# Small stages of an eight-step pass dealt anew over the matrix engine's queue

## The chip, the cores and the metric

The kernel runs on one core of a Trainium2 chip. The metric is the device time of one execution in microseconds (us); lower is better. The core has a matrix engine (TensorE, PE in the profile, with its weight loads as PEld), VectorE (DVE), ScalarE (ACT), GpSimd (POOL) and SyncE (SP). Each works through its own queue in the written order, and they wait for one another by semaphores.

## The reference

Two transformer layers over x of 8 batches, 512 tokens, 128 features, with a layer norm ahead of each part:

```python
x = x + _L0_attn_ref(_layernorm(x), Wq, Wk, Wv, g_scale)   # 16 heads of 8; q, k to unit length
x = x + _L0_ffn_ref(_layernorm(x), ...)                    # top-1 of 8 experts, hidden 32, gelu
x = x + _L1_attn_ref(_layernorm(x), w_q, w_k, w_v, w_o)    # 16 heads of 64, causal
x = x + _L1_ffn_ref(_layernorm(x), ...)                    # top-2 of 8 experts, hidden 512, gelu
```

The first attention is softmax(g q k^T) v with unit q and k ("cosine" scores); the second is causal softmax(q k^T / 8) v and a projection. The first expert layer computes a hidden row with gelu for all experts, masks it by the chosen one, and multiplies by W2; the second sorts the rows by expert.

## The kernel before

Everything but the second expert layer runs in one software pipeline. `steps()` gives passes i = -3 to 8 of eight steps, p = 0 to 7. In a pass the second attention is at batch l1 = i, one **pair** of heads a step; the first expert layer is at batch f = i+1; the first attention at s = i+2, two **portions** (`cosine` 0 and 1, 128 keys of four heads each) a step; layer norm and projections of the first attention at h = i+3; and routing of the second expert layer at t = i-1. So passes -2 and -1 have portions but (nearly) no pairs, passes 0 to 5 have both, 6 and 7 have pairs alone. Behind the pipeline the second expert layer runs over sorted rows; the change doesn't touch it.

The order is written out by hand, once for each engine, in four loops over `steps()` that must agree. On PE a step is:

- `score_unit(g, 0)` and `max_unit(g+1, 0)`; `values0(c-1)`, the weighted values of the portion before;
- `values1(g-1)` in two halves, with `cosines(c)`, the scores of the step's first portion, between them;
- score and max unit 1, then small stages ("fills"); score and max unit 2; the q projection of pair g+2;
- more fills; `sums1` (denominators of pair g-1), `max_transposed` (row maxima of pair g+1), the k projection;
- `cosines(c+1)`, `values0(c)`, and a tail of fills, after which the next step begins.

Fills are, among others, `values1_rows` (the second attention's values, eight pieces (t, half) for a batch, three matmuls each), `transposes` to "xtT", "xh2T", "xnT", "xT0", "x2T", `logits0`, `hidden0`, `onehot_transposed`, `masks0` and `experts0_out` of the first expert layer, `qkv0` of the first attention, `group_operands` (its qT and kT), `projection_out`, and `logits1` and `ranks1` of the routing.

Two resources tie the order down. Score, max and cosine units alternate between two PSUM slots (`UNIT_NO`, from `unit_order`): a unit waits until the unit two before it has been read, by ACT's exponentials (`score_exp`, `cosine_exp`) or DVE's `maxima`. All projections and fills alternate between two other banks (`WORK_NO`, from `work_order`): `work_open` waits until the work two before it has been moved out:

```python
def work_open(pe, *name):
    pe.wait_ge(work_free[WORK_NO[name] % 2], work_fills(*name))
```

q and k are freed late: ACT writes their high part (`hi_part`, tile ra), then DVE the low part (`lo_part`, ra too, L1078). ACT has one activation table at a time; `hidden0_gelu` in step 3 loads the Gelu table, runs two Gelus, and loads the table of exponentials back. `group_rows`, `squares`, `unit_rows`, `variances`, `standardize`, `experts0_choice`, `routing1` are DVE stages. `parts_copied` (ACT) and `parts_split` (DVE) prepare `group_operands`.

## Time and profile before

| | before |
|---|---|
| time, median of 3 runs | 1633.49 us (1622.28 to 1648.9) |
| the profiled execution: its own time, its span | 1636.53 us, 1634.8 us |
| busy PE, PEld | 1327.0 us (81%), 798.3 us (49%) |
| busy DVE, ACT, POOL | 934.6 us (57%), 851.8 us (52%), 600.4 us (37%) |
| mean granted PE clock | 0.917 |

The span is the stretch that the profile shows instruction by instruction; the execution's own time is 1.7 us longer. A busy PE is one that has matmuls in its pipeline. Passes 0 to 7 lie between 167.77 us and 1365.60 us of the span, eight steps each; the pass taken as the sample below is pass 2, from 475.88 us to 632.78 us.

### The profile page before, as it was taken

What the parts mean: (1) busy time and instruction counts of PE and PEld (TensorE: products, weight loads), DVE (VectorE), ACT (ScalarE), POOL (GpSimd) and SP (SyncE); (2) the same over time, 40 slices, a digit from 0 to 9 for tenths busy, and PEclk for the clock granted to TensorE, in tenths of its full rate; (3) what the DMA queues carried; (4) which work ended last, traced back from release to release, by engine and by line L of the source; (5) the groups of instructions that cost most, each with busy time, mean ns of one, the idle gap of its engine ahead of it and who ended that gap; (6) DMA issues with size and microseconds to landing.
All of it is one profiled execution on the core that took longest, in us unless ns stands there. A gap on an engine that the chain in (4) does not pass through costs nothing.

```text
span 1634.8 us, 27815 instructions
## 1 busy us (share of the span) xinstructions
PE 1327.0 (81%) x9189; PEld 798.3 (49%) x9189; DVE 934.6 (57%) x3262; ACT 851.8 (52%) x1642; POOL 600.4 (37%) x768
## 2 busy tenths in 40 slices
PE   3878888988888789889988988988888884599970
PEld 1223444554455445545445444544555553488860
DVE  5355755565756576656555764555554654265655
ACT  3665665656565556555654665444424531255533
POOL 1010322233253335333423442235325444265554
PEclk7878999999999999989998999899979987699985
DMA  7060990000000000000000000001010000212222
GB/s 288 1 229 1 8 3 1 1 7 8 1 14 8 7 1 21 1 7 3 19 1 8 8 8 1 7 8 59 8 43 36 1 11 22 90 54 55 58 90 104
DMA packets 63051, 53.17 MB, mean 33 GB/s; under 512 B 39752, under 2 KB 49488, under 8 KB 62656
## 3 DMA queue, kind: packets, MB, share of 16 engines
q1 hardware_dynamic: 58592, 42.47, 13.2%
q0 software_dynamic: 4320, 8.92, 1.6%
q8 instruction: 78, 1.28, 0.3%
q14 instruction: 61, 0.50, 0.1%
HBM read 20.56 MB, written 30.81 MB: 31 GB/s over the span
## 4 chain that ended last, share of the span: by engine, by line
PE 59%; DVE 17%; ACT 14%; issue 7%; POOL 2%; DMA 1%; POOLq 1%; SPq 0%; DVEq 0%; ACTq 0%
PE scores L1529 10%; PE work L1469 8%; PE outs L1675 7%; PE outs L1548 6%; DVE scores L1085 5%; ACT a_buf L824 5%; PE work L1578 4%; PE scores L1498 3%; DVE ra L1078 3%; PE scores L1662 3%; PE work L1561 3%; ACT ra L830 3%; PE outs L1860 2%; ACT rsum L836 2%; PE work L1559 2%
## 5 line engine op out<-in xcount | busy, mean ns | idle before, releaser
L1085 DVE CUSTOM_DVE_ANT_0 scores<-scores,mask_qk 128x512 f32<-128x512 f32 (+3 forms) x512 | 239.3, 520 | 240.8 <-PE scores L1498 238.1
L824 ACT ACTIVATE a_buf<-scores 128x1024 f32<-128x1024 f32 x256 | 248.0, 1026 | 110.7 <-PE scores L1662 101.4
L676 POOL TENSOR_SCALAR_AFFINE_SELECT big<-big 128x256 f32<-128x256 f32 x256 | 100.9, 407 | 541.5 <-ACT big L818 540.7
L818 ACT ACTIVATE big<-scores 128x1024 f32<-128x1024 f32 (+1 forms) x192 | 169.2, 882 | 231.0 <-PE scores L1529 224.5
L1529 PE MATMUL scores<-ra 64*128 64x512 f32 (+3 forms) x1536 | 188.8, 352 | 47.2 <-ACT a_buf L824 33.0
L686 POOL TENSOR_TENSOR big<-big 128x768 f32<-128x768 f32 x64 | 118.6, 1854 | 191.2 <-PE work L1561 191.0
L1529 PEld LDWEIGHTS scores<-ra 64*128 64x128 f32 x1536 | 124.4, 193 | 109.4 <-ACT a_buf L824 42.3
L1548 PE MATMUL outs<-big 128*64 128x512 f32 (+3 forms) x1024 | 164.8, 449 | 2.2 <-DVE yT L1109 2.2
L1675 PE MATMUL outs<-a_buf 128*16 128x512 f32 x1024 | 148.4, 655 | 8.6 <-DVE wqkv_lo L1032 4.9
L1109 DVE TENSOR_TENSOR yT<-outs,rsum 128x512 f32<-128x512 f32 x64 | 44.3, 692 | 148.4 <-ACT rsum L841 148.4
L1548 PEld LDWEIGHTS outs<-big 128*64 128x64 f32 x1024 | 64.2, 137 | 115.9 <-issue 103.4
L973 ACT ACTIVATE big<-scores,b_sb 128x128 f32<-128x128 f32 x284 | 81.1, 368 | 74.8 <-PE scores L1850 43.5
L669 POOL TENSOR_TENSOR rstd<-var_eps,minus_half 128x4 f32<-128x4 f32 x48 | 50.5, 1052 | 161.9 <-DVE var_eps L1047 161.9
L830 ACT CAST ra<-work 128x512 fp32r<-128x512 f32 x128 | 75.0, 586 | 61.7 <-PE work L1469 59.3
L773 POOL DMA_INDIRECT choice_rows<-big x71 | 69.7, 982 | 81.6 <-DVE big L1410 79.7
L1078 DVE TENSOR_TENSOR ra<-work,ra 128x512 fp32r<-128x512 f32 x128 | 87.9, 687 | 18.1 <-ACT ra L830 12.7
L1498 PE MATMUL scores<-ra 64*128 64x512 f32 (+3 forms) x512 | 81.6, 355 | 14.1 <-DVE neg_max L1085 13.1
L836 ACT ACTIVATE rsum<-work 128x512 f32<-128x512 f32 x64 | 38.2, 597 | 101.7 <-PE work L1561 101.7
L1529 PE MATMUL scores<-neg_max_T,pick 64*128 64x512 f32 (+3 forms) x512 | 85.7, 329 | 0.0
L1662 PE MATMUL scores<-qkT 32*128 32x512 f32 x512 | 74.3, 516 | 12.8 <-ACT a_buf L824 10.5
L689 POOL TENSOR_TENSOR big<-big 128x512 f32<-128x512 f32 x64 | 82.4, 1288 | 5.0
L1469 PE MATMUL work<-x_hi,wqkv_hi 128*128 128x512 f32 x128 | 67.7, 529 | 20.0 <-ACT rsum L836 19.8
(216 smaller groups left out, 2600.7 us busy)
## 6 DMA issues: line engine op xcount, KB each, us to landing
sorted_rows<-xrows SPq DMA_DIRECT2D x33, 520.0 KB, 6.8
big<-sorted_rows SPq DMA_DIRECT2D x71, 65.0 KB
a_buf<-in_w SPq DMA_DIRECT2D x2, 2048.0 KB, 8.2
a_buf<-choice_rows SPq DMA_DIRECT2D x16, 256.0 KB, 4.9
a_buf<-in_x SPq DMA_DIRECT2D x8, 256.0 KB, 2.9
x_rows<-x SPq DMA_DIRECT2D x8, 256.0 KB, 2.0
ra<-x_rows SPq DMA_DIRECT2D x8, 256.0 KB
out<-a_buf SPq DMA_DIRECT2D x8, 256.0 KB, 2.0
```

The costliest lines, as they stand in the source:

```text
L686: nc.gpsimd.tensor_tensor(tsum, prob1(g, 0)[:, :, P:SEQ], prob1(g, 1)[:, :, 0:3 * P], ALU.add).then_inc(tsum_step, 1)
L818: activation(prob1(g, i), d[:, :, 0:256] if i == 2 else d, ACT.Exp, scale=SCALE1).then_inc(unit_free("pair", g, i), 1)
L824: activation(prob0(c)[:, i * 1024:(i + 1) * 1024], unit_wait(act, "cosine", c, i), ACT.Exp).then_inc(unit_free("cosine", c, i), 1)
L830: copy(dst[:, g % 2, :], w).then_inc(qk1_hi, 1)
L1078: v.tensor_tensor(lo[:, g % 2, :], w, hi[:, g % 2, :].bitcast(F32), ALU.subtract).then_inc(free_of(which, g), 1)
L1085: return v.tensor_tensor_reduce(scores_, scores_, mask_qk[:, SEQ - width:SEQ], -1.0, 3e38, ALU.add, ALU.min, neg_max[:, qt, j:j + 1])
L1469: last = mm(dst, a, c, start=(n == 0), stop=(n == 2))
L1498: last = mm(d[:, j * SEQ + at:j * SEQ + at + width], q_hi[heads(j), g % 2, qt * P:(qt + 1) * P], k_hi[heads(j), g % 2, 0:width], start=(n ...
L1529: last = mm(d[:, j * SEQ + at:j * SEQ + at + width], lhs, c[heads(j), g % 2, queries], start=(n == 0 and term == 0), stop=(n == len(blocks ...
L1548: last = mm(outs[heads(j), 0, kb * P:], v1[:, kb, n * D1:(n + 1) * D1], probs, start=(kb == 0), stop=(kb == TILES - 1))
L1662: last = mm(d[:, i * SEQ:(i + 1) * SEQ], qkT0[rows, 1, g % 2, kb * P:(kb + 1) * P], qkT0[rows, 0, g % 2, :], start=True, stop=True)
L1675: last = mm(outs[STRIP * j:STRIP * j + VCOLS, 1, :], vstat(s)[:, kb, g * HG + j, :], prob0(c)[:, j * SEQ:(j + 1) * SEQ], start=(kb == 0), ...
```

## The change

Only the order is changed; every stage remains, with the same operands. It does the following:

- **A new place for fills** right behind `values0(c-1)`, ahead of `values1`. In steps 0 to 7 it holds: v(3,0); v(1,1); lg0; nothing; both masks; qkv0 0 and 1; v(0,0); v(1,0).
- **At most one fill between q and the sums**: v(0,1); xtT; xh2T; xnT; lg1; qkv0 3; none; none.
- **Behind unit 1**: oT in the even steps, and v(2,1), v(3,1), qkv0 2, v(2,0) in the odd ones.
- **`values0(c)` moves** from behind `cosines(c+1)` to ahead of the k projection.
- **Step 3 (`GELU_STEP`)**: `cosines(c)` and its exponentials move behind score and max unit 1.
- **Tails**: ohT in step 3, xT0 in step 4 behind `experts0_out`, rank in step 5 behind x2T. On DVE `routing1` comes behind the additions of y0, `slots1` and `gates1` move to step 6, `unit_rows` to the middle of step 7. On ACT `parts_copied` moves from early in steps 1, 3, 5 to the end of steps 0, 2, 4, and in step 7 from early to behind the exponentials of unit 1; `inverse_norms` moves from the end of step 6 to early in step 7.

```diff
+GELU_STEP = 3
...
@@ unit_order
-        units += cosine(0) if i == 0 else []
+        units += cosine(0) if i == (1 if o.p == GELU_STEP else 0) else []
@@ scalar
-                if p in (1, 3, 5) and s is not None:
-                    parts_copied(s, p // 2 + 1)
-                if p == 7 and h is not None:
-                    parts_copied(h, 0)
-                if p == 3 and f is not None:
+                if p == GELU_STEP and f is not None:
                     hidden0_gelu(f)
...
+                if p == 7 and h is not None:
+                    inverse_norms(h)
-                if o.cosine(0) is not None:
+                if o.cosine(0) is not None and p != GELU_STEP:
                     cosine_exp(o.cosine(0))
...
+                if o.cosine(0) is not None and p == GELU_STEP:
+                    cosine_exp(o.cosine(0))
...
+                if p in (0, 2, 4) and s is not None:
+                    parts_copied(s, p // 2 + 1)
                 if (o.i, p) == (-2, 0):
                     weights_hi_parts()
@@ vector
-                if p == 4 and t is not None:
-                    routing1(t)
                 if p == 4 and f is not None:
                     for i in range(2):
                         w = work_wait(dve, "y0", f, i)
...
+                if p == 4 and t is not None:
+                    routing1(t)
@@ tensor
+                if p == 0 and l1 is not None:
+                    values1_rows(l1, 3, 0)
+                if p == 1 and l1 is not None:
+                    values1_rows(l1, 1, 1)
+                if p == 2 and f is not None:
+                    logits0(f)
+                if p == 4 and f is not None:
+                    masks0(f, 0)
+                    masks0(f, 1)
+                if p == 5 and h is not None:
+                    qkv0(h, 0)
+                    qkv0(h, 1)
...
                 if o.pair(1) is not None:
                     max_transposed(o.pair(1))
+                if o.cosine(0) is not None:
+                    values0(o.cosine(0))
                 if o.pair(2) is not None:
                     project("k", 1, o.pair(2))
                 if o.cosine(1) is not None:
                     cosines(o.cosine(1))
-                if o.cosine(0) is not None:
-                    values0(o.cosine(0))
```

**Step 3 on PE**, from `values0` to score unit 2, of the pass with i = 1; before (`scores<-qkT` is a portion's scores, `outs<-a_buf` is `values0`, `outs<-big` `values1`, `scores<-ra` score and max units, `work<-wqkv` a piece of v):

```order
506 L1675 MATMUL outs<-a_buf 16x512 x4
507 L1548 MATMUL outs<-big 64x512 x2
508 L1548 MATMUL outs<-big 64x384 x2
509 L1662 MATMUL scores<-qkT 128x512 x4
510 L1548 MATMUL outs<-big 64x256 x2
511 L1548 MATMUL outs<-big 64x128 x2
512 L1529 MATMUL scores<-ra 128x384 x6
```

and after:

```order
522 L1556 MATMUL outs<-big 64x128 x2
523 L1537 MATMUL scores<-ra 128x384 x6
524 L1537 MATMUL scores<-neg_max_T,pick 128x384 x2
525 L1537 MATMUL scores<-ra 128x128 x6
526 L1537 MATMUL scores<-neg_max_T,pick 128x128 x2
527 L1506 MATMUL scores<-ra 128x384 x2
528 L1506 MATMUL scores<-ra 128x128 x2
529 L1477 MATMUL work<-wqkv_hi,x_hi 128x512
530 L1477 MATMUL work<-wqkv_lo,x_hi 128x512
531 L1477 MATMUL work<-wqkv_hi,x_lo 128x512
532 L1670 MATMUL scores<-qkT 128x512 x4
533 L1537 MATMUL scores<-ra 128x256 x6
```

The portion's scores stood ahead of unit 1 and now stand behind it and a piece of v.

**The end of step 3 on PE**, from the denominators to the next step; before (`work<-big,ones` is `sums1`, L1509 `max_transposed`, L1469 the k projection, L1648 `group_operands`):

```order
529 L1559 MATMUL work<-big,ones 64x128 x2
530 L1561 MATMUL work<-big,ones 64x384 x2
531 L1509 MATMUL work<-ident_b,neg_max_hl 128x128 x4
532 L1469 MATMUL work<-x_hi,wqkv_hi 128x512
533 L1469 MATMUL work<-x_lo,wqkv_hi 128x512
534 L1469 MATMUL work<-x_hi,wqkv_lo 128x512
535 L1662 MATMUL scores<-qkT 128x512 x4
536 L1675 MATMUL outs<-a_buf 16x512 x4
537 L1648 MATMUL work<-ident_r,parts 128x128 x8
538 L1469 MATMUL work<-wqkv_hi,x_hi 128x512
```

and after:

```order
540 L1567 MATMUL work<-big,ones 64x128 x2
541 L1569 MATMUL work<-big,ones 64x384 x2
542 L1517 MATMUL work<-ident_b,neg_max_hl 128x128 x4
543 L1683 MATMUL outs<-a_buf 16x512 x4
544 L1477 MATMUL work<-x_hi,wqkv_hi 128x512
545 L1477 MATMUL work<-x_lo,wqkv_hi 128x512
546 L1477 MATMUL work<-x_hi,wqkv_lo 128x512
547 L1670 MATMUL scores<-qkT 128x512 x4
548 L1656 MATMUL work<-ident_r,parts 128x128 x8
549 L1621 MATMUL work<-ident_b,a_buf 8x128 x4
```

`values0` now stands ahead of the k projection, and the operands' transposes come straight behind the portion's scores.

**The first two steps of pass -2 on PE**, where there are no pairs; before:

```order
3 L1648 MATMUL work<-ident_r,parts 128x128 x8
4 L1662 MATMUL scores<-qkT 128x512 x8
5 L1675 MATMUL outs<-a_buf 16x512 x4
6 L1462 MATMUL outs<-bias_ln_sb,res 128x8 x2
7 L1675 MATMUL outs<-a_buf 16x512 x4
8 L1662 MATMUL scores<-qkT 128x512 x8
9 L1675 MATMUL outs<-a_buf 16x512 x4
```

and after:

```order
3 L1656 MATMUL work<-ident_r,parts 128x128 x8
4 L1670 MATMUL scores<-qkT 128x512 x4
5 L1683 MATMUL outs<-a_buf 16x512 x4
6 L1670 MATMUL scores<-qkT 128x512 x4
7 L1470 MATMUL outs<-bias_ln_sb,res 128x8 x2
8 L1683 MATMUL outs<-a_buf 16x512 x4
9 L1670 MATMUL scores<-qkT 128x512 x4
10 L1683 MATMUL outs<-a_buf 16x512 x4
```

The scores of two portions stood together (x8); now each is followed by its own `values0`.

**ACT in the same place**; before:

```order
18 L824 ACTIVATE a_buf<-scores 128x1024 x4
19 L802 CAST wqkv_hi<-yT 128x2048
20 L804 CAST wqkv_hi<-yT 128x1024
21 L852 CAST parts<-a_buf 128x4x16 x4
22 L852 CAST parts<-a_buf 128x8x8 x4
```

and after:

```order
18 L831 ACTIVATE a_buf<-scores 128x1024 x4
19 L859 CAST parts<-a_buf 128x4x16 x4
20 L859 CAST parts<-a_buf 128x8x8 x4
21 L809 CAST wqkv_hi<-yT 128x2048
22 L811 CAST wqkv_hi<-yT 128x1024
```

The copies of the parts now stand ahead of the high parts of the weights.

## Rows read from the trace of the kernel before

**Rows 1.** Page, part 4: the chain that ended last, shares of the span.
```profile
PE 59%; DVE 17%; ACT 14%; issue 7%; POOL 2%; DMA 1%; POOLq 1%; SPq 0%; DVEq 0%; ACTq 0%
```
**Rows 2.** Windows: steps 0 to 7 of pass 2; length, busy by engine, clock, DMA.
```profile
475.88:492.00 16.12, 14.07 (x108) 7.27 (x107) 8.62 (x27) 9.34 (x14) 8.83 (x12) 1.00 0.05 17
492.00:512.86 20.86, 18.85 (x145) 11.79 (x145) 14.62 (x62) 12.30 (x23) 8.44 (x10) 1.00 0.05 15
512.86:532.10 19.24, 17.11 (x124) 9.17 (x123) 11.49 (x42) 9.69 (x13) 6.37 (x8) 1.00 0.01 1
532.10:554.35 22.25, 17.32 (x121) 9.99 (x121) 12.84 (x50) 15.26 (x26) 7.53 (x9) 0.92 0.00 1
554.35:578.09 23.74, 20.11 (x150) 12.05 (x150) 14.56 (x51) 10.38 (x14) 6.89 (x11) 1.00 0.03 12
578.09:596.68 18.59, 16.46 (x119) 8.42 (x118) 11.45 (x48) 12.62 (x29) 6.38 (x8) 1.00 0.00 1
596.68:616.22 19.54, 17.74 (x138) 10.88 (x138) 15.45 (x46) 10.88 (x16) 7.63 (x9) 1.00 0.01 4
616.22:632.78 16.56, 15.00 (x114) 8.04 (x113) 8.29 (x31) 11.22 (x22) 7.69 (x10) 1.00 0.04 13
```
**Rows 3.** Timeline, step 1: start, length, engine, line; [idle before it <- what ended it].
```profile
502.11 0.39 PE L1469 MATMUL work<-wqkv_hi,x_hi 128*128 128x512 f32 x1
...
503.67 0.44 PE L1559 MATMUL work<-big,ones 128*64 128x128 f32 x4 [0.72 <-DVE ra L1078]
...
504.69 0.40 PE L1509 MATMUL work<-ident_b,neg_max_hl 128*128 128x128 bf16 x4
...
505.45 0.50 PE L1469 MATMUL work<-x_hi,wqkv_hi 128*128 128x512 f32 x1 [0.37 <-ACT rsum L836]
...
506.34 0.51 PE L1662 MATMUL scores<-qkT 32*128 32x512 f32 x4
...
506.78 1.05 PE L1675 MATMUL outs<-a_buf 128*16 128x512 f32 x8
...
506.93 1.95 ACT L824 ACTIVATE a_buf<-scores 128x1024 f32<-128x1024 f32 x2
507.12 0.68 DVE L1078 TENSOR_TENSOR ra<-work,ra 128x512 fp32r<-128x512 f32 x1
...
509.09 3.84 PE L1578 MATMUL work<-wo_sb,yT 128*128 128x128 f32 x32 [0.45 <-DVE qkT L1131]
```
**Rows 4.** Timeline, step 3: the Gelu on ACT and what PE waits for.
```profile
534.26 1.25 ACT L852 CAST parts<-a_buf 128x64 fp32r<-128x64 f32 x8
...
535.53 1.28 ACT L877 ACT_TABLE_LOAD   x1
...
536.82 1.26 ACT L877 ACTIVATE a_buf<-work,bias 128x512 f32<-128x512 f32 x2
...
539.40 1.94 ACT L824 ACTIVATE a_buf<-scores 128x1024 f32<-128x1024 f32 x2
...
540.47 1.16 PE L1529 MATMUL scores<-ra 64*128 64x384 f32 x6 [3.07 <-ACT a_buf L824]
```
**Rows 5.** Timeline, step 4: a transpose's wait, the routing's first row, the last fill's wait.
```profile
563.88 0.63 PE L1476 MATMUL work<-ident_r,a_buf 128*128 128x128 f32 x4 [1.45 <-DVE attn L1142]
...
572.67 0.18 DVE L1062 TENSOR_REDUCE top<-lg 128x4 f32<-128x32 f32 x1
...
577.27 0.89 PE L1588 MATMUL work<-wqkv_sb,a_buf 128*128 128x384 f32 x2 [0.25 <-DVE res L1332]
```
**Rows 6.** Timeline, pass -2: PE's wait for the weights, four exponentials in a row.
```profile
39.15 1.91 PE L1675 MATMUL outs<-a_buf 128*16 128x512 f32 x8 [4.86 <-DVE wqkv_lo L1032]
...
49.87 3.77 ACT L824 ACTIVATE a_buf<-scores 128x1024 f32<-128x1024 f32 x4 [4.19 <-PE scores L1662]
```
**Rows 7.** Windows: behind the Gelu's wait in pass 2, and step 4 of pass 3.
```profile
540.47:544.48 4.01, 4.01 (x23) 3.29 (x23) 1.21 (x5) 1.89 (x2) 0.65 (x2) 0.57 0.00 0
711.23:737.36 26.13, 22.97 (x149) 13.30 (x148) 14.30 (x51) 10.52 (x14) 6.91 (x11) 0.87 0.03 11
```

More of the change, by code:

```diff
@@ L101, in add @@
             names.extend(some)
-    if p in (0, 2, 4, 6):
-        b, g = (s, p // 2 - 1) if p else (f, GROUPS0 - 1)
-        add(b, ("oT", b, g))
-    if p == 1:
-        add(l1, ("v", l1, 0, 1))
-    if p == 3:
-        add(l1, ("v", l1, 2, 1))
-    if p == 4:
-        add(f, ("mask", f, 0))
-        add(h, ("xT0", h))
-    if p == 5:
-        add(t, ("rank", t))
-        add(h, ("qkv0", h, 1))
-    if p == 7:
-        add(f, ("v", f, 1, 0))
-    add(o.pair(2), ("q", o.pair(2)))
     if p == 0:
@@ L125, in work_order @@
     if p == 2:
-        add(f, ("xtT", f), ("xh2T", f))
-    if p == 3:
-        add(t, ("xnT", t))
-        add(f, ("ohT", f))
+        add(f, ("lg0", f))
     if p == 4:
-        add(f, ("mask", f, 1))
-        add(t, ("lg1", t))
+        add(f, ("mask", f, 0), ("mask", f, 1))
     if p == 5:
-        add(h, ("qkv0", h, 2), ("qkv0", h, 3))
+        add(h, ("qkv0", h, 0), ("qkv0", h, 1))
     if p == 6:
@@ L137, in work_order @@
     if p == 7:
-        add(f, ("v", f, 2, 0))
+        add(f, ("v", f, 1, 0))
+    if p in (0, 2, 4, 6):
+        b, g = (s, p // 2 - 1) if p else (f, GROUPS0 - 1)
+        add(b, ("oT", b, g))
+    if p == 1:
+        add(l1, ("v", l1, 2, 1))
+    if p == 3:
+        add(l1, ("v", l1, 3, 1))
+    if p == 5:
+        add(h, ("qkv0", h, 2))
+    if p == 7:
+        add(f, ("v", f, 2, 0))
+    add(o.pair(2), ("q", o.pair(2)))
+    if p == 0:
+        add(l1, ("v", l1, 0, 1))
+    if p == 1:
+        add(f, ("xtT", f))
+    if p == 2:
+        add(f, ("xh2T", f))
+    if p == 3:
+        add(t, ("xnT", t))
+    if p == 4:
+        add(t, ("lg1", t))
+    if p == 5:
+        add(h, ("qkv0", h, 3))
     add(o.pair(-1), ("sum", o.pair(-1)))
@@ L149, in work_order @@
     if p == 2:
-        add(f, ("lg0", f), ("hid0", f, 0), ("hid0", f, 1))
+        add(f, ("hid0", f, 0), ("hid0", f, 1))
     if p == 3:
-        add(l1, ("v", l1, 3, 1))
+        add(f, ("ohT", f))
     if p == 4:
         add(f, ("y0", f, 0), ("y0", f, 1))
-        add(h, ("qkv0", h, 0))
+        add(h, ("xT0", h))
     if p == 5:
         add(f, ("x2T", f))
+        add(t, ("rank", t))
     if p == 6:
@@ L1262, in _ @@
                     squares(h)
+                if p == 7 and h is not None:
+                    unit_rows(h)
                 if o.pair(1) is not None:
@@ L1313, in _ @@
                     work_moved(dve, "projB", t)
-                if p == 2 and f is not None:
-                    w = work_wait(dve, "lg0", f)
-                    v.tensor_copy(lg0[:], w[:, 0:TILES * EXPERTS].rearrange(
-                        "p (t e) -> p t e", e=EXPERTS)).then_inc(free_of("lg0", f), 1)
                 if p == 2 and t is not None:
@@ L1343, in _ @@
                                     ALU.subtract).then_inc(free_of("x2T", f), 1)
-                if p == 6 and h is not None:
-                    unit_rows(h)
+                if p == 5 and t is not None:
+                    ranks_moved(t)
+                if p == 6 and t is not None:
+                    slots1(t)
+                    gates1(t)
                 if p == 6 and l1 is not None:
@@ L1755, in _ @@
                     max_unit(o.pair(1), 2)
-                if p == 6 and f is not None:
-                    work_moved(pe, "x2T", f)
                 if o.pair(2) is not None:
@@ L1779, in _ @@
                 if p == 5 and h is not None:
-                    qkv0(h, 2)
                     qkv0(h, 3)
-                if p == 6 and f is not None:
-                    values1_rows(f, 0, 0)
-                if p == 7 and f is not None:
-                    values1_rows(f, 2, 0)
                 if o.pair(-1) is not None:
@@ L1793, in _ @@
                     cosines(o.cosine(1))
-                if o.cosine(0) is not None:
-                    values0(o.cosine(0))
                 if p in (1, 3, 5) and s is not None:
@@ L1810, in _ @@
                 if p == 4 and h is not None:
-                    qkv0(h, 0)
+                    pe.wait_ge(rows_ready["a0"], h + 1)
+                    transposes(rows_h, "xT0", h)
                 if p == 5 and f is not None:
@@ L1814, in _ @@
                     transposes(rows_a, "x2T", f)
+                if p == 5 and t is not None:
+                    ranks1(t)
                 if p == 6 and l1 is not None:
```

101 lines of the change are left out of this document (47 added, 54 removed).

## The prediction

> **What bounds the kernel now.** I read the chain of waits first [rows 1]: it runs over PE for 59% of the span, over DVE for 17% and over ACT for 14%. So PE's queue is the spine, and the rest is handshakes in which PE stands still for a DVE or ACT step. Next the windows of one pass, step by step [rows 2]: 156.9 us together, of which PE is busy 136.7 us. The 20.2 us left are spread over all steps (1.6 us in step 7, 2.1 in step 0), with two lumps: step 3 has 22.25 - 17.32 = 4.9 us and step 4 has 3.6 us. Then the timeline, to see what each hole is [rows 3 to 5]. In every step a few are the same:
>
> - q to sums: a fill starts at 502.11, the sums at 503.67, since with one fill between they share q's bank and wait for its low part on DVE. The hole is 1.56 us wide whatever fills it; a piece of v leaves 0.72 of it idle, so it costs about 0.84 [rows 3].
> - 0.37 us ahead of k, for the logarithm that frees the sums' bank [rows 3].
> - Behind unit 1, where PE waits for the exponentials of that unit: a hole of about a fill, filled in either kernel in most steps.
> - The Gelu step: ACT goes through parts 1.25, table 1.28, two Gelus 1.26, a table of the same length again, and only then the portion's exponentials, which PE's unit 1 needs: 3.07 us idle [rows 4].
>
> A hole is paid once, so a fill in it is free and the same fill elsewhere costs its length. That is how I price a change that only moves things. All step sums are against the lengths in [rows 2].
>
> **The change part by part.**
>
> *`values0(c)` ahead of k.* The transposed maxima start at 504.69 and k at 505.45, 0.76 us later with 0.37 idle [rows 3]. With `values0` between (the operands start 0.98 after it begins; its row says 1.05, modelled end), k starts 0.38 + 0.98 = 1.36 later: +0.60. The tail loses 0.98. Net -0.38 wherever the tail is pure work. But `values0` used to hide something: k's low part is done on DVE at 507.12 + 0.68 = 507.80, 2.35 us after k begins, and the second of the exponentials' halves later still [rows 3]. In a step with no tail (step 0) the next score unit waited for the first half of the exponentials before and waits as long now: they begin at 506.93, 1.48 behind k's start, one half is 0.97, so 2.5 to 2.7 us behind k in both kernels; there the move is a plain +0.6. With operands in the tail, kT waits for the low part, at 2.4 instead of 1.8 behind k. In step 1 the projection then waits for DVE's copy of qT, begun when the low part is done: 2.35 + 0.7 + 0.05 = 3.1 against 509.09 - 505.45 = 3.64: -0.54, after +0.6.
>
> *Fills behind the values.* Nothing is waited for there, so a fill costs its length: 0.8 for a piece of v, 0.9 for lg0, 0.7 for both masks, 1.7 for two pieces qkv0. It pays only where it empties a place in which it cost as much or more.
>
> Step by step:
> - Step 0: v(3,0) +0.8, v(0,1) is free in the q hole as v(3,0) was, `values0` +0.6: **+1.4**.
> - Step 1: v(1,1) +0.8, v(2,1) and xtT in holes, `values0` +0.6 - 0.54: **+0.9**.
> - Step 2: lg0 only changes place; xtT is gone from a q hole that held two fills (the second waits for the low part and then costs its length): -0.6; `values0` -0.38, and 0.1 back where the second hidden matmul waits for k's low part: **-0.9**.
> - Step 3: PE's unit 1 no longer waits. It starts at about 4.9 us of the step (540.47 - 532.10 = 8.4, less 3.07 idle, less 0.44 for the portion's scores). On ACT, with the parts gone, loads and Gelus end at 6.1, unit 1's exponential at 7.2. The portion's scores follow, and DVE must have read max unit 1 by 8.2. Then comes a new wait, with nothing of PE's between: the two exponentials of the portion [rows 4], the first free at 8.8 for score unit 2, the second at 9.8 for max unit 2. So I leave 1.6 us idle there, 1.0 in the later holes and 0.4 at the start. Work: 17.32, less v(2,1) 0.7, less 1.3 that the slower clock had added (below): 15.3. Sum 18.35: **-3.9**. Queued behind the late portion on ACT are unit 2's exponential and q's high part; both come in time, since q begins at 10.1.
> - Step 4: xT0 waited 1.45 us for DVE in the bank of oT [rows 5]; it now stands in the tail. The routing stood on DVE from 572.67 for 4 us ahead of the additions of y0, and PE's qkv0 came at 577.27 behind these [rows 5]; the additions now come first and PE doesn't wait for them. Work 20.11 less one qkv0 0.85 = 19.3, waits left 1.5 (unit 1 and 2 about 0.5, q hole 0.6, small ones): 20.8: **-2.9**. The routing still takes its 4 us, and holds DVE's first maxima of step 5 until 5.4 us of that step; they are needed there by the second half of the portion's scores at 5.9, since two qkv0 stand ahead. So it is covered by 0.5 us.
> - Step 5: work 16.46 + 0.85, waits 2.3 (rank at the end waits for DVE's copy of kT, 3.8 behind k): 19.6: **+1.0**.
> - Step 6: v(0,0) +0.8; no fill between q and sums, so the sums go at once, and only the maxima wait for the low part (q to k 3.8 instead of 4.1 with `values0` inside): -0.4; tail -1.0: **-0.6**.
> - Step 7: v(1,0) +0.8, same -0.4, kT's wait leaves the tail at 2.9 instead of 3.2; ACT's parts, 1.25, stand ahead of unit 2's exponential and delay q's high part by 0.2: **+0.4**.
>
> Sum -4.6 us a pass (156.9 to 152.3). Passes 0 to 5 are of this kind: **-27.6**. Passes 6 and 7 have no portions; fills at the new place cost there, the emptied holes pay: **-2**, between -6 and +4.
>
> *The start.* Passes -2 and -1 have portions and few pairs, so ACT's exponentials set the pace: four in a row, 3.77 us, when two portions' scores are issued together [rows 6]. Now the second portion's scores stand behind `values0` of the first, which waits for both its exponentials: per step ACT idles for 0.98 + 0.44 + 0.1, about 1.5 us, where no fills lie between. Four steps are light enough for the full price, but where qT and kT, weights or xT0 kept PE busy anyhow it is 0 to 1. Against that, step 7 of pass -2 no longer holds ACT behind the norms: I give it -3. One item is certain: in step 0 of pass -2 the weights' high parts come behind the later exponentials and the parts. PE already waits 4.86 us for them [rows 6]; later exponentials 2.5 plus parts 1.25: +3.7. The start in all: **+5.5**, between 0 and +18.
>
> *The clock.* Behind the 3.07 us wait the granted clock over 540.47 to 544.48 is 0.57 [rows 7], most of it at 1.2 GHz. That cost is in step 3 above. There is more: step 4 of pass 3 took 26.13 at 0.87, against 23.74 in pass 2 [rows 7]. I take four such losses of 2.4 us for passes 3 to 5. With fewer and shorter idle stretches I expect half of them gone: **-5**, between -10 and 0. The Trainium skill, TensorE: Matmul & The Clock Gate, Part 1, says that the throttled level is the default and that activity lifts it; the trace agrees in step 3, where a wait precedes the fall, but in step 4 of pass 3 no wait as long stands ahead.
>
> The sum: -27.6 - 2 + 5.5 - 5 = -29 us. The profiled execution is 1636.5 us, 3 us above the median of the runs, so it becomes 1607.4, and the median **1604 us** (-1.8%).
>
> A place where page and row differ: the switch of tables. The row shows 1.28 us and the Gelu starting right behind it [rows 4]. The Trainium skill, ScalarE: Activation LUTs, What ACT_TABLE_LOAD costs, adds a drain of 1380 ns to each switch. By that, the exponential of unit 1 in step 3 would end 2.8 us later and an estimated 2.8 x 6 = 17 us of the gain would be gone. The row decides, and I add nothing.
>
> **The rivals.**
>
> *A cleaner clock* (0.2): with the longest wait gone all losses of that kind vanish and the start is as cheap as its lower end: -27.6 - 4 + 1 - 10 = -41: 1593. For it: the fall in [rows 7] follows the wait. Against: the falls in later passes.
>
> *The Gelu step keeps DVE on the path* (0.12): ahead of the maxima of unit 1, which free the slot for the portion's second half, stand `experts0_choice` and the variances. If they end 2 us later than I reckon, everything behind shifts: -29 + 6 x 2 = -17: 1616. That would be the change not doing what it says.
>
> *The start at its worst* (0.12): 12 steps at 1.5 us, and a good part at half clock since PE idles more: -29 + 18 = -11: 1622.
>
> *Slower* (0.06): `values0` was a buffer behind k; without it there are bare waits of about 1 us behind k in steps 0, 1, 3, 5 and 7 and 1.6 us in step 3. If these drop the clock once or more a pass, each fall costs some 2.4 us (26.13 - 23.74) [rows 7]. The gain is used up at 29 / 2.4 = 12 falls, two a pass; at three a pass the sum is +14: 1647.
>
> **How the numbers follow.** The forecast has 0.5, and its own bounds (passes 6 and 7, the start, fill prices of 0.7 or 0.84 in four steps) are about 12 us to each side. The range holds the cleaner clock, the Gelu and the start's rivals: 1586 to 1632. 2%, about what a measurement of this kernel can tell from no change, is 32.7 us: faster means below 1600.8. All of the first rival and 0.4 of the forecast's half lie below: 0.40. Slower by over 2% needs 1666, past even the slow rival: 0.03. The rest 0.57.
>
> **What would show it.** The windows of a pass: 152 us in place of 157, step 3 at 18 to 19, step 4 at 21, but steps 0, 1 and 5 longer by 1 us each. The row of unit 1 in step 3 without a wait on ACT; in its place up to 1 us ahead of score unit 2. No 0.37 ahead of k; a wait of 0.5 ahead of kT. Pass -2 with exponentials in twos and the weights' wait above 8 us. If step 3 is still over 20, or the start over 10 us longer, or the granted clock below 0.9, the prediction is wrong at that term.

## The result: 1.8% slower, and where the time went

| | before | after |
|---|---|---|
| time, median | 1640.13 us (4 runs, 1622.28 to 1648.9) | 1657.93 us (4 runs, 1652.76 to 1662.49) |
| ratio, 95% interval | | 1.0184 (1.0099 to 1.0268) |
| profiled execution, its span | 1636.53, 1634.8 us | 1652.76, 1651.0 us |
| busy PE, DVE | 1327.0, 934.6 us | 1335.9, 966.5 us |
| mean granted PE clock | 0.917 | 0.909 |

The changed kernel is slower by 1.0 to 2.7%. (The ratios leave out executions in a slower state of the chip, so they differ from the quotients of the medians (1.011 here), and of one experiment, a_weights, the profiled execution was among those slower ones, so only its start is read from the trace.) The prediction said 1604 us with a range of 1586 to 1632. The chain of the page has moved from PE and ACT to DVE, against [rows 1]:

```profile
PE 53%; DVE 20%; ACT 11%; issue 9%; POOL 4%; POOLq 1%; DMA 1%; SPq 0%; DVEq 0%; ACTq 0%
```

Next I cut each span into four stretches: passes -2 and -1 (from 30 us), passes 0 to 5, passes 6 and 7, and what lies behind the pipeline. The columns are those of [rows 2]. Of after:

```profile
30.00:196.47 166.47, 118.31 (x585) 44.72 (x585) 70.94 (x252) 86.75 (x165) 5.11 (x5) 0.65 0.17 67
196.47:1132.97 936.50, 823.91 (x5947) 461.20 (x5947) 599.76 (x2036) 542.95 (x908) 332.86 (x421) 0.98 0.12 7
1132.97:1378.14 245.17, 208.26 (x1460) 133.81 (x1461) 137.21 (x472) 104.17 (x157) 115.79 (x145) 0.92 0.08 28
1378.14:1651.00 272.86, 176.97 (x1176) 153.28 (x1174) 143.85 (x454) 108.48 (x390) 133.21 (x175) 0.83 0.23 70
```

And of before:

```profile
30.00:167.77 137.77, 108.33 (x586) 41.86 (x587) 70.74 (x252) 86.76 (x165) 6.53 (x5) 0.78 0.21 81
167.77:1113.01 945.24, 822.58 (x5947) 463.94 (x5947) 566.49 (x2036) 544.03 (x908) 338.30 (x419) 0.97 0.12 7
1113.01:1365.60 252.59, 212.66 (x1461) 136.53 (x1462) 139.07 (x472) 103.91 (x157) 116.74 (x146) 0.90 0.08 27
1365.60:1634.80 269.20, 174.59 (x1175) 151.26 (x1174) 143.58 (x454) 108.33 (x390) 133.23 (x175) 0.82 0.23 71
```

| stretch | change | forecast |
|---|---|---|
| start | 166.47 - 137.77 = +28.7 | +5.5 |
| passes 0 to 5 | 936.50 - 945.24 = -8.7 | -27.6, and -5 for the clock |
| passes 6 and 7 | 245.17 - 252.59 = -7.4 | -2 |
| behind | 272.86 - 269.20 = +3.7 | 0 |

The sum is +16.3 us, and the two executions differ by 1652.76 - 1636.53 = 16.2. The forecast was -29, so the miss is 45 us: 23 of it in the start and 24 in passes 0 to 5. In both the counts of instructions are the same within a few, so it is the same work: in the start PE is busy 10 us longer at a clock of 0.65 for 0.78, and in passes 0 to 5 **DVE is busy 33 us longer** (599.76 for 566.49). The second is the odd one: moving instructions should not lengthen them.

The steps of pass 2, after, against [rows 2]:

```profile
507.09:524.67 17.58, 14.89 (x109) 7.75 (x109) 8.45 (x27) 9.60 (x14) 7.30 (x10) 1.00 0.04 13
524.67:546.28 21.61, 19.61 (x148) 12.22 (x148) 14.96 (x62) 12.68 (x24) 7.56 (x10) 1.00 0.05 14
546.28:564.69 18.41, 16.72 (x119) 8.73 (x118) 11.48 (x42) 9.19 (x13) 6.38 (x8) 1.00 0.01 1
564.69:583.72 19.03, 17.04 (x120) 9.64 (x119) 11.95 (x50) 15.26 (x27) 6.92 (x9) 0.91 0.00 0
583.72:604.41 20.69, 19.36 (x149) 11.83 (x147) 11.60 (x35) 9.26 (x13) 7.05 (x11) 1.00 0.04 14
604.41:625.81 21.40, 17.71 (x121) 9.28 (x121) 17.62 (x64) 13.13 (x31) 6.38 (x8) 0.98 0.00 1
625.81:645.95 20.14, 18.94 (x139) 11.55 (x139) 12.57 (x41) 10.47 (x14) 6.30 (x8) 0.94 0.00 1
645.95:664.47 18.52, 15.39 (x113) 8.01 (x113) 14.37 (x37) 11.95 (x24) 10.25 (x13) 1.00 0.06 19
```

Steps 0 to 2 and 4 are within 0.2 us of their forecast, step 3 within 0.7 (it takes 19.03 us here at a clock of 0.91, and 18.14 us in passes 1, 3 and 5, where its clock is 1.00). Steps 5, 6 and 7 are 1.8, 1.2 and 1.6 us over it, and DVE is busy 17.62 us in step 5 and 14.37 in step 7. The timeline of step 7 shows with what. L693, L696 and L699 are `sum_blocks` on POOL, L1129 is `parts_split` on DVE, L1656 the operands' transposes on PE:

```profile
658.23 1.82 POOL L693 TENSOR_TENSOR big<-big 128x768 f32<-128x768 f32 x1 [0.74 <-PE work L1569]
658.38 4.38 DVE L1129 TENSOR_TENSOR parts<-a_buf,parts 128x64 fp32r<-128x64 f32 x8
...
660.13 1.28 POOL L696 TENSOR_TENSOR big<-big 128x512 f32<-128x512 f32 x1
...
661.49 0.73 POOL L699 TENSOR_TENSOR big<-big 128x256 f32<-128x256 f32 x1
...
662.82 0.53 PE L1656 MATMUL work<-ident_r,parts 128*128 128x128 f32 x4 [1.51 <-DVE parts L1129]
```

The same step before, same view:

```profile
627.74 1.16 DVE L1120 TENSOR_TENSOR parts<-a_buf,parts 128x64 fp32r<-128x64 f32 x8
...
629.06 1.82 POOL L686 TENSOR_TENSOR big<-big 128x768 f32<-128x768 f32 x1 [2.89 <-PE work L1561]
```

Before, DVE had finished its eight subtractions, 1.16 us, 0.16 us ahead of POOL's first addition. After, POOL is released 0.15 us ahead of them, and they take 4.38 us: until POOL's three additions are over. POOL's own rows are as long as before. Windows inside each of the three additions show which instructions of the group are under way there, one in each:

```profile
658.38 1.75 DVE L1129 TENSOR_TENSOR parts<-a_buf,parts 128x64 fp32r<-128x64 f32 x1
660.19 1.30 DVE L1129 TENSOR_TENSOR parts<-a_buf,parts 128x64 fp32r<-128x64 f32 x1
661.55 0.74 DVE L1129 TENSOR_TENSOR parts<-a_buf,parts 128x64 fp32r<-128x64 f32 x1
```

So three of the eight subtractions stand, and each ends 0.08 us behind the addition that it met (658.38 + 1.75 = 660.13, POOL's first ends at 658.23 + 1.82 = 660.05).

In step 5 it is `standardize` (L1063); the timeline, and behind it the chain of waits through that place and into step 6 (start, length, what):

```profile
618.52 4.31 DVE L1063 TENSOR_SCALAR a_buf<-res,mean,rstd 128x128 f32<-128x128 f32 x4
...
618.77 1.83 POOL L693 TENSOR_TENSOR big<-big 128x768 f32<-128x768 f32 x1 [2.62 <-PE work L1569]
...
624.09 0.54 PE L1656 MATMUL work<-ident_r,parts 128*128 128x128 f32 x4 [2.31 <-DVE ra L1087]
```

```profile
620.61 2.23 DVE a_buf L1063 x2
622.84 0.60 DVE yT L1118
623.44 0.60 DVE ra L1087
624.03 0.61 DVE qkT L1140
...
625.82 2.07 PE scores L1537 x8
```

Behind `standardize` stand the normalization of the outputs, k's low part and the copy of qT, so PE waits 2.31 us ahead of kT. Step 6 then begins at a clock below 1 (its first scores take 2.07 us, 1.12 in step 5), and the windows give it 0.94.

The start is another matter. The chain of waits of after, pass -2:

```profile
47.40 1.91 PE outs L1683 x8
49.31 0.74 PE scores L1670 x2
...
50.08 1.95 ACT a_buf L831 x2
...
52.16 1.91 PE outs L1683 x8
...
89.16 0.45 PE scores L1670 x2
...
89.63 1.95 ACT a_buf L831 x2
...
91.71 1.05 PE outs L1683 x8
92.77 0.45 PE scores L1670 x2
```

One portion after the other: values, scores, two exponentials, values. A round takes 52.16 - 47.40 = **4.76 us** where the matmuls take 1.91 and 0.74, which is the 1.2 GHz level, and 92.77 - 89.16 = 3.61 us at 2.4 GHz. From 42.65 to 82.61 us every round is of the first kind (granted clock 0.50). A few rounds at 2.4 GHz follow, and from 98.93 to 155.97 us the mean is 0.55 again.

### The profile page after: what moved, and what is told of

It reads as the page before. It is cut to its first block, busy times and chain, and to the rows that moved or that the text cites. A ratio compares the mean times of both kernels' runs of the same rounds, so it can differ in the third digit from the quotient of the medians.

```text
span 1651.0 us, 27815 instructions
## 1 busy us (share of the span) xinstructions
PE 1335.9 (81%) x9189; PEld 797.5 (48%) x9189; DVE 966.5 (59%) x3262; ACT 851.3 (52%) x1642; POOL 592.5 (36%) x768
## 3 DMA queue, kind: packets, MB, share of 16 engines
q8 instruction: 78, 1.28, 0.3%
## 4 chain that ended last, share of the span: by engine, by line
PE 53%; DVE 20%; ACT 11%; issue 9%; POOL 4%; POOLq 1%; DMA 1%; SPq 0%; DVEq 0%; ACTq 0%
PE scores L1537 9%; PE work L1477 8%; PE outs L1683 8%; ACT a_buf L831 6%; PE outs L1556 6%; DVE scores L1094 6%; PE work L1586 4%; PE scores L1506 4%; DVE ra L1087 3%; ACT ra L837 3%; PE scores L1670 3%; DVE parts L1129 2%; PE work L1569 2%; POOL big L768 2%; DVE a_buf L1063 1%
## 5 line engine op out<-in xcount | busy, mean ns | idle before, releaser
L1683 PE MATMUL outs<-a_buf 128*16 128x512 f32 x1024 | 155.0, 680 | 42.7 <-ACT a_buf L831 34.3
L693 POOL TENSOR_TENSOR big<-big 128x768 f32<-128x768 f32 x64 | 117.0, 1828 | 150.7 <-PE work L1569 150.5
L1556 PE MATMUL outs<-big 128*64 128x512 f32 (+3 forms) x1024 | 161.0, 443 | 2.2 <-DVE yT L1118 2.2
L982 ACT ACTIVATE big<-scores,b_sb 128x128 f32<-128x128 f32 x284 | 81.1, 368 | 75.7 <-PE scores L1863 40.1
L696 POOL TENSOR_TENSOR big<-big 128x512 f32<-128x512 f32 x64 | 82.2, 1285 | 5.0
L843 ACT ACTIVATE rsum<-work 128x512 f32<-128x512 f32 x64 | 38.2, 597 | 79.4 <-PE work L1569 79.3
L1873 PE MATMUL outs<-a_buf,big 128*128 x568 | 77.0, 280 | 0.8 <-ACT big L982 0.8
```

The lines of the kernel that those rows point to most:

```text
L693: nc.gpsimd.tensor_tensor(tsum, prob1(g, 0)[:, :, P:SEQ], prob1(g, 1)[:, :, 0:3 * P], ALU.add).then_inc(tsum_step, 1)
L1556: last = mm(outs[heads(j), 0, kb * P:], v1[:, kb, n * D1:(n + 1) * D1], probs, start=(kb == 0), stop=(kb == TILES - 1))
L1683: last = mm(outs[STRIP * j:STRIP * j + VCOLS, 1, :], vstat(s)[:, kb, g * HG + j, :], prob0(c)[:, j * SEQ:(j + 1) * SEQ], start=(kb == 0), ...
```

## The experiments

Two theories came out of this, one for each place. **The collision**: POOL's additions and DVE's instructions on SBUF tiles can't run side by side, and the emptied place between q and the sums lets POOL start 1.5 us earlier against DVE's group (0.15 ahead of it for 1.32 behind its start), and so into it. Rival: the steps are long since PE has lost its fills there and waits for q's low part. **The lone portions**: `values0` ahead of the second portion's scores turns pairs of portions into lone ones, with PE idle for nearly half of each round at the low clock. Rival: the weights' later high parts and the other moves in the start.

The times (before is measured again beside each set):

| run | time, us | before | ratio to before, 95% | pass 0 begins | passes 0 to 5 |
|---|---|---|---|---|---|
| before | | | | 167.77 | 945.2 |
| after | 1657.93 | 1640.13 | 1.0184 (1.0099 to 1.0268) | 196.47 | 936.5 |
| a_start | 1626.33 | 1642.4 | 0.9931 (0.9881 to 0.9981) | 163.05 | 941.4 |
| a_pool | 1626.42 | 1642.4 | 0.9923 (0.9882 to 0.9964) | 196.62 | 909.1 |
| a_both | 1594.18 | 1642.4 | 0.9725 (0.9633 to 0.9817) | 162.43 | 915.8 |
| b_gelu | 1618.55 | 1642.4 | 0.9890 (0.9845 to 0.9936) | 167.10 | 935.7 |
| b_single | 1669.82 | 1642.45 | 1.0163 (1.0107 to 1.0219) | 182.75 | 963.2 |
| b_lock | 1657.52, one run | 1642.45 | none | 166.50 | 969.3 |
| a_behind_k | 1589.23 | 1642.45 | 0.9672 (0.9623 to 0.9721) | 162.69 | 909.6 |
| a_mixed | 1593.72 | 1642.45 | 0.9697 (0.9646 to 0.9748) | 161.84 | 919.1 |
| a_weights | 1651.7 | 1635.29 | 1.0080 (1.0040 to 1.0120) | 193.93 | not read |
| a_best | 1588.7 | 1635.29 | 0.9709 (0.9660 to 0.9759) | 160.16 | 907.0 |

**a_start**: after, with `values0` back behind the second portion's scores where the step has no k projection.

```diff
-                if o.cosine(0) is not None:
+                if o.cosine(0) is not None and o.pair(2) is not None:
                     values0(o.cosine(0))
...
                     cosines(o.cosine(1))
+                if o.cosine(0) is not None and o.pair(2) is None:
+                    values0(o.cosine(0))
```

> The changed kernel with one edit on PE: in steps without a k projection (passes -2 and -1) values0 of the first portion stands behind the second portion's scores again. Theory 1: the start lost its 28.7 us because single portions leave PE too idle, so that it stays at the lower clock and each portion costs 4.75 us; then pass 0 begins near 170 to 176 us of the span instead of 196.5, and the time falls by 20 to 28 us, to about 1627 to 1635 us. Rival: it is the weights' high parts behind the exponentials and parts on ACT, and the other moves in passes -2 and -1; then pass 0 begins later than 188 us and the time falls by under 9 us.

Pass 0 begins at 163.05 us, 33.4 earlier than after, 4.7 earlier than before and also earlier than the 170 to 176 expected. The window of the start:

```profile
30.00:163.05 133.05, 103.93 (x586) 40.76 (x585) 70.59 (x252) 85.90 (x165) 5.16 (x5) 0.82 0.22 85
```

The same 586 matmuls, with the clock at 0.82 for 0.65. So one line in the wrong place for these two passes costs all of the +28.7 and 4.7 more, and the other moves of the change together help the start. About 5 us of it are lost again right behind the start: steps 0 and 1 of pass 0 take 40.1 us for after's 34.9, at clocks of 0.75 and 0.91 for 1.00.

**a_pool**: after, with `sum_blocks` held back on POOL in steps 5 and 7 until DVE's group is done.

```diff
+                ready = None
+                if p == 5 and f is not None:
+                    ready = (rows_ready["f0"], f * 3 + 3)
+                if p == 7 and h is not None:
+                    ready = (parts_ready, h * GROUPS0 + 1)
                 if o.pair(0) is not None:
-                    sum_blocks(o.g)
+                    sum_blocks(o.g, ready)
```

> The changed kernel with one edit on POOL: in step 5 its block sums wait until DVE has standardized the rows for x2T, in step 7 until DVE has split the parts; a wait is added and no work moved. Theory 2: POOL's block sums now start while DVE reads two SBUF operands or standardizes, and DVE's instructions stand still meanwhile (4.3 us in place of 1.1); then both DVE groups are back at 1.1 to 1.2 us, step 5 shortens by 1.8 us, step 7 by 1.5 us and step 6 by about 1.2 us since the clock no longer falls behind step 5's wait: together 4 to 4.5 us a pass in passes 0 to 4, 20 to 25 us of the time. Rival: DVE's groups are late because more stands ahead of them; then they stay above 3 us, or the wait of kT stays at 2.2 us, and the time doesn't fall.

Step 7, the rows that answer to those above (L1136 is `parts_split`, L695 the first addition, L1663 the transposes):

```profile
645.22 1.16 DVE L1136 TENSOR_TENSOR parts<-a_buf,parts 128x64 fp32r<-128x64 f32 x8
...
646.46 1.83 POOL L695 TENSOR_TENSOR big<-big 128x768 f32<-128x768 f32 x1 [2.13 <-DVE parts L1136]
...
648.07 0.53 PE L1663 MATMUL work<-ident_r,parts 128*128 128x128 f32 x4
```

4.38 us are 1.16 again and PE doesn't wait for the parts. In step 5 the wait ahead of kT is 0.50 us for 2.31. A wait was added and nothing removed, and steps 5, 6 and 7 fell by 1.9, 1.1 and 1.7 us; passes 0 to 5 by 27.4 us (20 to 25 expected). Over the six passes these three steps fell by 28.7 us, and the others, which differ only in the clock, rose by 1.3. The profiled executions differ by 38.2 us; the other 11 lie behind pass 5 and I don't count them as the edit's. Step 6 is not touched by the edit: it gains since its clock is at 1.00. The rival fails, since the fills are as in after.

Which DVE instructions stand can be read from after too. Of the subtractions `ra<-work,ra` 51 begin inside an addition of POOL and 77 outside, and of `yT<-outs,rsum` 50 and 14: the median is 0.69 us for all but the last 14, which have 0.68. Each of these has one input in PSUM (`work`, `outs`), as the casts `qkT<-work` have (0.68 us inside, 0.69 outside), and none is slowed.

The groups of instructions on DVE say the same of the whole program. `parts_split` in after (L1129) and in a_pool (L1136), mean ns of one behind the busy time:

```profile
L1129 DVE TENSOR_TENSOR parts<-a_buf,parts 128x64 fp32r<-128x64 f32 x256 | 59.2, 303 | 16.7 <-ACT parts L859 16.7
L1063 DVE TENSOR_SCALAR a_buf<-res,mean,rstd 128x128 f32<-128x128 f32 x64 | 35.8, 621 | 1.1 <-POOL rstd L676 1.1
```

```profile
L1136 DVE TENSOR_TENSOR parts<-a_buf,parts 128x64 fp32r<-128x64 f32 x256 | 40.5, 231 | 16.7 <-ACT parts L866 16.7
L1070 DVE TENSOR_SCALAR a_buf<-res,mean,rstd 128x128 f32<-128x128 f32 x64 | 18.3, 349 | 1.1 <-POOL rstd L676 1.1
```

**a_both**: the two edits together.

> Both edits together: PE's order of the passes without pairs as before the change, and POOL's block sums held back in steps 5 and 7. If both theories hold and add up, the changed kernel less 25 us at the start and less 22 us in the passes: near 1605 us, 1.5 to 2.5% faster than the kernel before. If they share a cause (the clock), less than 35 us together.

Its steps 5, 6 and 7 of pass 2:

```profile
562.92:582.42 19.50, 17.48 (x121) 8.95 (x121) 14.61 (x64) 13.41 (x31) 6.39 (x8) 1.00 0.00 1
582.42:601.49 19.07, 17.87 (x138) 10.90 (x139) 12.59 (x41) 10.20 (x14) 6.29 (x8) 1.00 0.01 1
601.49:618.27 16.78, 15.33 (x113) 8.01 (x112) 11.34 (x37) 11.34 (x24) 7.66 (x10) 1.00 0.05 17
```

The pass takes 151.9 us. That is the forecast's 152.3, step by step (below). Passes 1 to 5 take 151.8 to 154.2 us, the longer ones at a lower clock in step 3 or 4. By the medians a_start saves 31.6 us on after, a_pool 31.5 and a_both 63.7, so the two causes add up; the 1605 us expected are undercut by 11.

**b_gelu**: before, with the late portion of step 3 alone (`unit_order`, `scalar` and `tensor`).

```diff
-        units += cosine(0) if i == 0 else []
+        units += cosine(0) if i == (1 if o.p == 3 else 0) else []
```

> The kernel before with one part of the change: in step 3 the first portion's scores and exponentials stand behind score and max unit 1. By the prediction's reckoning the 3.07 us wait goes, a wait of up to 1 us comes ahead of score unit 2, and the slower clock behind it goes too: step 3 shortens from 22.3 to 19.5 to 20.5 us, so 2 to 3 us a pass, 12 to 18 us of the time. Rival: the parts' copies still stand ahead of the Gelu on ACT, and the wait only moves; then step 3 stays above 21.5 us and the time is the same within 6 us.

Faster by 0.6 to 1.5%. Step 3 of pass 2 takes 21.20 us for 22.25, which is neither the 19.5 to 20.5 expected nor the rival's 21.5. The 3.07 us ahead of unit 1 are gone, but PE now waits 2.07 us ahead of the portion's scores, for the exponential of unit 1 that stands behind the Gelu. It ends 8.3 us into the step, in after 7.2: the rival was partly right, since here the parts' copies (1.25 us) still stand ahead of the Gelu, and the change takes them away. What is left of that wait the change fills with a piece of v. So of the change's step 3 (19.03 us) the late portion alone gives about a third, and the other moves the rest.

Pass 2 isn't shorter for it: 157.06 us for 156.90, since step 4 takes 24.96 for 23.74, at a clock of 0.93 for 1.00. The profiled executions differ by 22.7 us, of which 9.5 lie in passes 0 to 5 and 10.9 in passes 6 and 7, which the edit doesn't touch. That the time fell by about the 12 to 18 us expected is therefore in good part luck with the clock.

**b_single**: before, with the opposite of a_start.

```diff
+                if o.cosine(0) is not None and o.pair(2) is None:
+                    values0(o.cosine(0))
                 if o.cosine(1) is not None:
                     cosines(o.cosine(1))
-                if o.cosine(0) is not None:
+                if o.cosine(0) is not None and o.pair(2) is not None:
                     values0(o.cosine(0))
```

> The kernel before with the reverse of the first edit: in steps without a k projection values0 of the first portion stands ahead of the second portion's scores, as in the change. If single portions alone keep PE at the lower clock at the start, the parts, the weights and the rest staying as before, pass 0 begins at 185 to 195 us of the span in place of 167.8, with values0 rows of 1.9 us through most of passes -2 and -1, and the time rises by 18 to 27 us. If the order of parts and weights on ACT was needed too, it begins before 178 us.

The start is 15.0 us longer (182.75 for 167.77), between the two ranges on record (185 to 195, or under 178), with rounds of 4.76 us as in after but for shorter stretches (mean clock of the start 0.75, after 0.65). PE's wait for the weights is 7.27 us, before 4.86. The rest was not expected: passes 0 to 5 hold the same instructions in the same order and take 18 us longer. One step shows where, step 4 of pass 2, which took 23.74 in before [rows 2]:

```profile
578.71:608.02 29.31, 26.14 (x151) 15.30 (x150) 14.37 (x51) 10.52 (x14) 6.88 (x11) 0.76 0.03 10
```

**b_lock**: before, with v(2,0) of step 7 taken from between q and the sums and put behind v(1,0), so that POOL starts early.

```diff
-    if p == 7:
-        add(f, ("v", f, 2, 0))
...
-        add(f, ("v", f, 1, 0))
+        add(f, ("v", f, 1, 0), ("v", f, 2, 0))
```

> The kernel before with v(2,0) of step 7 moved from between q and the sums to behind v(1,0), so that the sums of step 7 follow q at once. Theory 2: that alone lets POOL's block sums begin 1.5 us earlier, while DVE splits the parts; these eight instructions then take above 4 us in step 7 in place of 1.16, and kT waits about 2 us in a kernel that has nothing else of the change. Rival: the slow DVE groups come from what the change queued on DVE in steps 6 and 7 (slots, unit rows); then they stay at 1.2 us.

The collision can be made at will in the kernel before:

```profile
638.25 1.82 POOL L684 TENSOR_TENSOR big<-big 128x768 f32<-128x768 f32 x1 [1.01 <-PE work L1558]
638.40 4.38 DVE L1117 TENSOR_TENSOR parts<-a_buf,parts 128x64 fp32r<-128x64 f32 x8
...
642.84 0.54 PE L1645 MATMUL work<-ident_r,parts 128*128 128x128 f32 x4 [1.61 <-DVE parts L1117]
```

4.38 us again, step 7 takes 17.90 us for 16.56, with every stage in it the same; the 1.34 us hold the moved piece of v as well as the wait. In passes 0 to 4 that is 6.6 us; pass 5 has no parts in step 7, and the step is 1.0 us shorter there. Passes 0 to 5 took 24.0 us more in this one execution, and the other 18.4 are lower granted clock, most of it in steps 0, 3 and 4 (mean of the stretch 0.95 for 0.97).

**a_behind_k**: a_both with `values0` behind the second portion's scores in every step.

> The version with both edits, and values0 of the first portion behind the second portion's scores in all steps, as before the change. The prediction gave the move ahead of k +0.6 us in step 0, +0.06 in step 1 and -0.2 to -0.4 in the others. So steps 0 and 1 should be 0.6 and 0.1 us shorter than in the version with both edits, steps 2, 4 and 6 0.3 us longer, the pass within 1 us of its 150 to 152 us, and the time the same within 5 us. Rival: values0 as a buffer behind k is worth more than a bare hole, and the time falls by over 6 us; or the 0.37 us ahead of k cost every step, and it rises by over 6.

**a_mixed**: a_both with `values0` ahead of k only in steps 2 to 7, and the weights' high parts ahead of the operands' parts.

> The version with both edits, with values0 ahead of k only in steps 2 to 7, and the weights' high parts ahead of the parts' copies in step 0 of pass -2. Steps 0 and 1 lose 0.6 us together or a little more (6 passes: 4 us), the start 1.2 us: about 5 us less than the version with both edits, near 1590 us. If step 0 stays at 17.5 us, the prediction's reason for its +0.6 (the exponentials' first half ends no earlier) is wrong.

The two and a_both are within 5 us of each other, and their intervals overlap, so the times can't tell where `values0` should stand in a full pass. The steps of pass 1 can, in which a_both and a_behind_k have a clock of 1.00 throughout. With `values0` ahead of k step 0 is 0.55 us longer, as the prediction had it, and steps 2, 3 and 4 are 0.25, 0.12 and 0.40 shorter; but step 1 is 0.12 shorter instead of longer, steps 5 and 6 don't gain (within 0.1), and step 7 is 0.69 longer. The pass is 0.4 us longer by the move (151.77 for 151.35), where the expectation's terms add up to a gain of 0.5 to 1.7. a_mixed has step 0 at 17.02 us, which bears out the reason given for +0.6; its start is 0.6 us shorter than a_both's, not 1.2.

**a_weights**: after, with the weights' high parts ahead of the operands' parts and nothing else; it was to tell why the start costs 28.7 in after and 15.0 in b_single.

```diff
-                if p in (0, 2, 4) and s is not None:
-                    parts_copied(s, p // 2 + 1)
                 if (o.i, p) == (-2, 0):
                     weights_hi_parts()
+                if p in (0, 2, 4) and s is not None:
+                    parts_copied(s, p // 2 + 1)
```

> The changed kernel with one move on ScalarE: in step 0 of pass -2 the high parts of the weights are written ahead of the operands' parts, as the kernel before has them. Open is why pass 0 begins at 196.47 us in the changed kernel and only at 182.75 in the kernel before with single portions. Theory 1 (the lone portions hold the clock at 1.2 GHz for as long as they alternate, whatever stands ahead): only the length of the parts and their handshake comes back; values0 starts 1.2 us (the parts) to 3.5 us earlier than 42.65, the portions still take 4.76 us each, the mean clock from 30 us to pass 0 stays at 0.65 to 0.67, and pass 0 begins at 193 to 196 us. Theory 2 (the longer idle stretch at the weights, 8.4 us in place of 4.9, sets when the clock first rises): the portions go to 3.6 us each at some time ahead of 75 us, the mean clock is 0.70 or more, and pass 0 begins at 181 to 188 us. The passes behind it are as in the changed kernel, 157 us; the time is 1655 by theory 1 and 1645 by theory 2.

`values0` starts at 41.65 for 42.65, a little less than the 1.2 us expected; pass 0 begins at 193.93, the rounds stay at 4.76 us until 79.7 us, and the mean clock from 30 us on is 0.66. All this is theory 1's. PE's first wait is 7.27 us, as long as in b_single, where pass 0 begins 11 us earlier. So, as far as this one trace tells, the length of the first wait is not what parts the two.

**a_best**: a_behind_k with that move as well.

> The changed kernel with everything that has helped: values0 behind the second portion's scores in all steps, sum_blocks of steps 5 and 7 behind VectorE's standardize and parts_split, and the high parts of the weights ahead of the operands' parts in step 0 of pass -2. Against the kernel with the first two alone (1589 us) I expect the weights' wait 1.1 us shorter and nothing else: 1588 us, within 4 us, since the granted clock of step 3 or 4 of some passes differs from program to program. If the clock of the start follows the length of the first wait, 3 us more are gained there.

1588.7 us, a ratio of 0.9709 beside a_behind_k's 0.9672 in its own set: no difference that can be told. Both beat before by about 3%, and a_best beats after by 4% by the medians (1588.7 / 1657.93 = 0.958) or 5% by the ratios (0.9709 / 1.0184 = 0.953).

## Why the prediction was wrong

**The steps, right.** The forecasts of the eight steps were 17.5, 21.8, 18.3, 18.35, 20.8, 19.6, 18.9 and 17.0 us. With the collision taken out, a_both shows 17.55, 21.62, 18.43, 18.23, 20.68, 19.50, 19.07 and 16.78. As sums these hold: fills priced by whether a hole waits for them, the 3.07 us of the Gelu step, the bank of xT0, the routing behind the additions of y0. Most terms in them were not tested one by one, and where they were some are off and cancel: the move of `values0` costs step 7 0.69 us instead of gaining there, and the slower clock of step 3 is worth 0.9 us (19.03 - 18.14), not 1.3. The exact place of a wait did not always: the new wait of step 3 was to be 1.6 us ahead of score unit 2 and is 0.3 us there, with the rest at the sums and kT.

**"Step 5: ... waits 2.3 ... +1.0", "Step 6: ... the sums go at once" and "Step 7: ... same -0.4": failed.** I counted the emptied place between q and the sums as a gain, and asked on PE's queue alone what the earlier sums do. They release POOL. POOL's additions then begin inside DVE's group, and DVE stands for up to 3.2 us (4.38 - 1.16) with everything queued behind it. The prediction's sum put this at nothing. Its price was 1.8 + 1.2 + 1.6 = 4.6 us a pass over the forecast; the wait in a_pool took 27.4 us out of six passes. The trace of before could have warned: in step 7 DVE's group ends only 0.16 us ahead of POOL's start (the rows above), and in step 5 of pass 5 the two overlap, and `parts_split` takes 4.32 us there.

The Trainium skill, SBUF — State Buffer, section "SBUF: two separate sides", says that DVE and GpSimd share a pair of ports by an exclusive lock that is held for the whole instruction, when the DVE instruction runs in a two-port mode, or has two SBUF inputs while GpSimd's instruction reads SBUF. The runs agree for DVE's eight subtractions, which have two SBUF inputs, and POOL's additions, which read SBUF: one that meets an addition stands until that addition ends, the next passes in the gap, and POOL's rows keep their 1.8 us. `standardize` has one SBUF tensor and a mean and deviation for each row, and stands as well; whether by the page's second condition, no run here tells. An estimate by the page's rule would have had the missing term: POOL's rows are 1.82 + 1.28 + 0.73 = 3.8 us long, so a group that starts 0.15 us behind them stands for at most about 3.7 us; 3.2 were measured.

**"The start: +5.5, between 0 and +18": mis-sized.** The mechanism was named (the second portion's scores behind `values0` of the first, ACT idle between) and the weights' wait was right (+3.7 forecast, 42.65 - 39.15 = 3.5; b_single, which has the later exponentials but not the parts ahead of the weights, shows 41.43 - 39.15 = 2.3 of it). The price per step was taken at full clock, 0.98 + 0.44 + 0.1, while [rows 6] show `values0` at 1.91 us in that very stretch. At 1.2 GHz a lone portion costs 4.76 us. I had "a good part at half clock" only in the bound, and took -3 for the norms. Measured +28.7; of it a_start takes back all, b_single makes 15.0 of it alone. What decides how long the low clock lasts stays open: in after it holds until 82.6 us and from about 99 to 153 us, in b_single the rounds of 4.76 us come in shorter stretches. a_weights speaks against the length of the first wait, and no run separates the fills that the two kernels have between their portions.

**"The clock: -5": about right in sign.** Passes 3 to 5 of before hold 9.5 us more than three times pass 2 (159.3 + 160.3 + 160.6 - 3 x 156.9). In after they hold less than three times pass 2, 468.5 for 472.1. With the collisions' 27.4 us the forecast's -27.6 - 5 would be -5.2; -8.7 was measured. The size can't be tested: a_pool and a_both have the same order in passes 0 to 5 and take 36.2 and 29.4 us less than before, and the 7 us between them are clock.

**"Passes 6 and 7: -2, between -6 and +4": mis-sized**, -7.4. The granted clock rose from 0.90 to 0.92, and step 4 of pass 6 alone went from 22.67 us (clock 0.73) to 17.21 (1.00). How much of the -7.4 is the change's own stays open, as b_gelu, which leaves these passes as they are, takes 10.9 us less in them. The +3.7 behind the pipeline lies in code that the change doesn't touch; it went from -3 to +5 between the runs.

**The rivals.** "The start at its worst" came true and was exceeded. "Slower" had the right side and the wrong mechanism: of the bare waits behind k only step 3's goes with a lower clock in pass 2 (0.91), and not two falls a pass. What was missing is a rival in which an engine that PE doesn't wait for starts early and stops one that it does wait for.

## What to carry to other kernels

When a place on PE's queue is emptied, look at every engine that the work behind it releases, not only at PE: what starts earlier there, and beside what. If POOL's tensor instructions come to lie over a group on DVE that reads SBUF, let POOL wait for that group; a wait that holds POOL back by 1.0 and 1.4 us in two steps of a pass gave 27 us here. Price a move in a stretch at the clock that the stretch has, and keep independent pieces in pairs so that one fills the other's latency.
